# An audio front end on one core: layer 1 of its convolution stack with five products for two positions

## What is computed

```python
CONVS = [(128, 10, 5)] + [(128, 3, 2)] * 4 + [(128, 2, 2)] * 2     # channels, taps, stride
h = x[:, None, :]
for w, g, b, s in zip(conv_ws, ln_gs, ln_bs, strides):
    h = _conv1d(h, w, s)
    h = jnp.swapaxes(h, -2, -1)
    h = _fp32_layernorm(h, g, b)
    h = jnp.swapaxes(h, -2, -1)
    h = jax.nn.gelu(h, approximate=False)
```

## Time and profile before

| | |
|---|---|
| three runs | 2405.05, 2409.25, 2409.69 us; median 2409.25 |
| the profiled execution | 2401.78 us, span 2399.9 us |
| busy in the span | PE 2174.9 us (91%), DVE 1358.0 (57%), ACT 1133.1 (47%), POOL 861.3 (36%) |
| from 500 to 800 us | PE 297.08 us of 300, DVE 206.19, ACT 170.25, POOL 162.93; granted clock 1.00 |

### The profile page before, as it was taken

The page is one execution under the profiler, slowest core; times in us unless marked ns, Lnnn a source line. Parts: engine busy times, 40 slices in busy tenths (PEclk is TensorE's granted clock), DMA queues, the critical chain, the costliest instruction groups (busy, mean ns, idle before and its releaser), DMA issues. The chain is left out here.

```text
span 2399.9 us, 41759 instructions
## 1 busy us (share of the span) xinstructions
PE 2174.9 (91%) x14659; PEld 1945.7 (81%) x14659; DVE 1358.0 (57%) x3616; ACT 1133.1 (47%) x2203; POOL 861.3 (36%) x760
## 2 busy tenths in 40 slices
PE   2999999999999999999999995978697889969988
PEld 1888999999999998999999884977465566759988
DVE  4676667667667667667667652422486365542222
ACT  1655565655655565555555541322343465542320
POOL 4444555555555554554555531101330000000000
PEclk9999999999999999999999996999798799989989
DMA  5700000000000000000000202666000010119966
GB/s 160 238 4 4 4 4 4 6 7 4 8 6 4 7 6 4 9 6 4 9 4 1 65 1 73 188 166 176 20 20 0 26 52 39 52 41 329 331 202 222
DMA packets 102376, 150.39 MB, mean 63 GB/s; under 512 B 14724, under 2 KB 80174, under 8 KB 101548
## 3 DMA queue, kind: packets, MB, share of 16 engines
q1 hardware_dynamic: 78636, 118.36, 15.7%
q10 hardware_dynamic: 17984, 20.30, 2.6%
q0 software_dynamic: 5568, 9.27, 1.3%
HBM read 102.32 MB, written 45.50 MB: 62 GB/s over the span
## 5 line engine op out<-in xcount | busy, mean ns | idle before, releaser
L303 PE MATMUL banks<-t_wt,t_l 128*128 128x256 f32 (+1 forms) x2836 | 597.5, 350 | 0.0
L483 POOL TENSOR_TENSOR t_rstd<-t_var,t_minus_half 128x4 f32<-128x4 f32 (+1 forms) x379 | 367.1, 968 | 633.4 <-DVE t_var L412 632.0
L303 PEld LDWEIGHTS banks<-t_wt,t_l 128*128 128x128 f32 x2836 | 510.3, 192 | 51.9
L366 ACT ACTIVATE t_sq<-banks 128x512 f32<-128x512 f32 (+1 forms) x379 | 215.9, 570 | 560.4 <-PE banks L303 558.0
L420 DVE TENSOR_TENSOR t_yn<-banks,t_rstd 128x512 f32<-128x512 f32 (+1 forms) x379 | 249.0, 657 | 367.8 <-POOL t_rstd L483 366.7
L294 PE MATMUL banks<-t_wt,t_l 128*128 128x128 f32 x2836 | 385.7, 278 | 4.1 <-ACT t_l L384 2.9
L294 PEld LDWEIGHTS banks<-t_wt,t_l 128*128 128x128 f32 x2836 | 355.2, 193 | 13.8 <-ACT t_l L384 3.9
L489 POOL TENSOR_TENSOR t_zrstd<-t_zvar,t_minus_half 128x8 f32<-128x8 f32 x188 | 307.6, 1637 | 25.3 <-DVE t_zvar L447 25.3
L400 ACT ACTIVATE t_l<-banks,t_cols 128x512 f32<-128x512 f32 x376 | 286.4, 777 | 43.2 <-PE banks L356 39.7
L384 ACT ACTIVATE t_l<-banks,t_cols 128x512 f32<-128x512 f32 (+1 forms) x381 | 284.8, 747 | 13.6 <-PE banks L316 8.3
L409 DVE TENSOR_REDUCE t_ss<-t_sq 128x4 f32<-128x512 f32 (+1 forms) x379 | 244.6, 645 | 80.9 <-ACT t_sq L366 74.0
(11 more groups left out here) (330 smaller groups left out, 3581.1 us busy)
## 6 DMA issues: line engine op xcount, KB each, us to landing
t_w<-in_w SPq DMA_DIRECT2D x64, 480.0 KB
t_w<-in_w SPq DMA_DIRECT2D x27, 576.0 KB, 5.1
ect<-t_ECT SPq DMA_DIRECT2D x16, 750.0 KB, 3.2
t_l<-in_w1a SPq DMA_DIRECT2D x27, 384.0 KB, 5.4
sorted_by_expert<-t_h SPq DMA_DIRECT2D x4, 2400.0 KB, 11.1
routed_by_expert<-t_h SPq DMA_DIRECT2D x4, 2400.0 KB, 17.7
t_ectb<-ect ACTq DMA_DIRECT2D x5, 1500.0 KB, 8.0
t_w1x<-in_w1x SPq DMA_DIRECT2D x64, 97.5 KB
```

The source lines that it names most:

```text
L303: mm = pe.matmul(psY[bank][:, t * C:end * C], src[:, at:at + P], weights[:, C:(1 + end - t) * C], start=False, stop=(t + 1 == n))
L366: act.activation(T["sq"][:, par, 0:n], psY[bank][:, 0:n], ACT.Square).then_inc(S["squared"], 1)
L483: pool.tensor_tensor(T["rstd"][:, par, 0:n], T["var"][:, par, 0:n], T["minus_half"][:, 0:n], ALU.pow)\
```

## The change

Layer 1 is written as y(m) = W1 o(m) + (W0+W2) e(m) + W0 (e(m-1) - e(m)) for an even tile of a pair, and the same with W2 (e(m+1) - e(m)) for the odd one. The product (W0+W2) e(m) serves both. So PE does five products of 128 columns for two tiles in place of six.

- POOL computes the differences of layer-0 tiles (`differences`, five parts per chunk into `dif`), ahead of the roots of g5, g6, g7 and of g0 and g1.
- PE writes the two shared products of a group to a `psL` bank, ACT copies them to SBUF (`read_shared`), DVE adds them into the group's `psY` bank in place (`add_shared`, ahead of the normalise of the group before).
- In g0 to g3 ACT does the gelu ahead of the square, which now waits for the addition.
- The small DVE instruction that makes the variance goes: the squares are scaled on ACT, and epsilon stands in a 129th column that the sum takes in.
- `STEP_AT` has other places; `v` has room for two batch entries, with two waits for scatters.

```diff
 def conv(pe, j, g):
+    if g < WG:
+        pair_products(pe, j, g)
...
+def pair_products(pe, j, g):
+    for p in range(2):
+        at = tap(1, out_blocks(1, half)[2 * p], 2)
+        mm = pe.matmul(psL[par][:, p * C:(p + 1) * C], T["l0"][:, at:at + P], T["wsum"][:, :], start=True, stop=True)
+    mm.then_inc(S["shared_done"], 1)
+    pe.wait_ge(S["normed"], count(j, g) - BANKS)
+    pe.wait_ge(S["dif_ready"], 5 * j + (3, 3, 4, 5)[g])
+    for t, m in enumerate(out_blocks(1, half)):
+        o, at = psY[bank][:, t * C:(t + 1) * C], tap(1, m, 1)
+        pe.matmul(o, T["l0"][:, at:at + P], T["wt"][:, 0, :], start=True, stop=False)
+        mm = pe.matmul(o, T["dif"][:, half, t * P:(t + 1) * P], T["wt"][:, 2 - t % 2, :], start=False, stop=True)
...
 def stats(dve, e):
-    dve.reduce_sum(T["ss"][:, par, 0:n], T["sq"][:, par, 0:n * C].rearrange("p (t c) -> p t c", c=C), axis=AX.X)\
-        .then_inc(S["summed"], 1)
-    dve.wait_ge(S["summed"], number)
-    dve.tensor_scalar(T["var"][:, par, 0:n], T["ss"][:, par, 0:n], 1.0 / C, EPS, ALU.mult, ALU.add)\
-        .then_inc(S["var_ready"], 1)
+    dve.reduce_sum(T["var"][:, par, 0:n], T["sq"][:, par, 0:n, :], axis=AX.X).then_inc(S["summed"], 1)
...
+def read_shared(act, j, g):
+    act.wait_ge(S["shared_done"], sums(j, g))
+    act.activation(T["shared"][:, par, :], psL[par][:, 0:2 * C], ACT.Copy).then_inc(S["shared_read"], 1)
...
+def add_shared(dve, j, g):
+    dve.wait_ge(S["shared_read"], sums(j, g))
+    dve.wait_ge(S["conv_done"], number)
+    dve.tensor_tensor(y, y, shared, ALU.add).then_inc(S["added"], 1)
...
-STEP_AT = [-1, 0, 1, -1, 2, 3, 4, -1, 5, 6, 7, 8, 9, 10, 11, 12, -1, 13, 14, 15, -1, 16, 17, 18, -1, 19, 20, 21, 22, 23, -1, 24, 25,
+STEP_AT = [0, -1, 1, -1, 2, 3, 4, -1, 5, 6, 7, -1, 8, 9, 10, -1, 11, 12, -1, 13, 14, 15, 16, 17, 18, -1, 19, 20, 21, 22, 23, 24, 25,
...
         for j in range(CHUNKS):
             for g in range(NG):
+                if g < 2:
+                    differences(pool, j, g + 2)
+                if g >= 5 and j + 1 < CHUNKS:
+                    differences(pool, j + 1, (0, 1, 4)[g - 5])
                 root(pool, event(j, g))
```

More of the change, by code:

```diff
@@ L205, in _ @@
                 .then_inc(S["wt_centred"], 1)
+            dve.wait_ge(S["wt_centred"], 1)
+            dve.wait_ge(S["w0_split"], 1)
+            dve.tensor_tensor(T["wsum"][:, :], T["wt"][:, 1, :], T["wt"][:, 2, :], ALU.add)
         @block.tensor
@@ L352, in layer0 @@
             pe.wait_ge(S["patch_copied"], 2 * c + i // 4 + 1)
-        if not isinstance(c, int) or 8 * c + i >= 2:
+        if c >= 1 and i < 2:
+            pe.wait_ge(S["shared_read"], sums(c - 1, 2 + i))
+        if 8 * c + i >= 2:
             pe.wait_ge(S["l0_ready"], 8 * c + i - 1)
@@ L361, in square @@
     def square(act, e):
-        layer, _, bank, par, number, _ = e
+        layer, half, bank, par, number, _ = e
         n = tiles(layer) * C
-        act.wait_ge(S["conv_done"], number)
+        if layer == 1:
+            act.wait_ge(S["added"], sums(number // NG - 1, half))
+        else:
+            act.wait_ge(S["conv_done"], number)
         act.wait_ge(S["summed"], number - 2)
-        act.activation(T["sq"][:, par, 0:n], psY[bank][:, 0:n], ACT.Square).then_inc(S["squared"], 1)
+        act.activation(T["sq"][:, par, 0:tiles(layer), 0:C], psY[bank][:, 0:n].rearrange("p (t c) -> p t c", c=C), ACT.Square,
+                       scale=C ** -0.5).then_inc(S["squared"], 1)
     def gelu(act, e, carry=None):
@@ L480, in root @@
         n = tiles(layer)
-        pool.wait_ge(S["var_ready"], number)
+        pool.wait_ge(S["summed"], number)
         pool.wait_ge(S["normed"], number - 2)
@@ L484, in root, with differences @@
             .then_inc(S["rstd_ready"], 1)
+    def differences(pool, j, part):
+        l0 = T["l0"]
+        out = T["dif"][:, part % 4, :].rearrange("p (t c) -> p t c", c=P)
+        even = lambda m: l0[:, block_at(0, m):block_at(0, m) + P]
+        if part == 0:
+            pool.wait_ge(S["conv_done"], count(j - 1, 3))
+        pool.wait_ge(S["l0_ready"], 8 * j + (1, 3, 5, 7, 7)[part])
+        if part == 4:
+            at = block_at(0, POS - 2) - 1
+            pool.tensor_tensor(out[:, 0, :], l0[:, at:at + P], even(0), ALU.subtract).then_inc(S["dif_ready"], 1)
+            return
+        if part == 0:
+            pool.tensor_tensor(out[:, 1, :], even(2), even(0), ALU.subtract)
+            pairs, o = view(l0[:, :], [[4 * BLOCK, 2], [1, P]], block_at(0, 2)), out[:, 2:4, :]
+            middle = view(l0[:, :], [[0, 2], [1, P]], block_at(0, 4))
+        else:
+            pairs = view(l0[:, :], [[4 * BLOCK, 2], [4 * BLOCK, 2], [1, P]], block_at(0, 8 * part - 2))
+            middle = view(l0[:, :], [[4 * BLOCK, 2], [0, 2], [1, P]], block_at(0, 8 * part))
+            o = out.rearrange("p (a b) c -> p a b c", a=2)
+        pool.tensor_tensor(o, pairs, middle, ALU.subtract).then_inc(S["dif_ready"], 1)
     def patch_root(pool, c, part):
@@ L1458, in _ @@
                     patch_root(pool, c, part)
+            for part in (0, 1, 4):
+                differences(pool, 0, part)
             for j in range(CHUNKS):
                 for g in range(NG):
+                    if g < 2:
+                        differences(pool, j, g + 2)
+                    if g >= 5 and j + 1 < CHUNKS:
+                        differences(pool, j + 1, (0, 1, 4)[g - 5])
                     root(pool, event(j, g))
```

71 lines of the change are left out of this document (51 added, 20 removed).

## The result

The changed kernel takes 2463.24 us (median of four runs, 2462.46 to 2469.31) against 2408.06 before: a ratio of 1.0236, interval 1.0216 to 1.0256, or 55 us slower. I had forecast 2428, with a range of 2396 to 2458. The profiled execution took 2462.60 us with a span of 2460.8, so 61 us more than the one before, where my sum said 19.

What follows compares the result with a forecast made beforehand. DVE and POOL handing work to and fro would bind: five periods +17 us, first six chunks +2, last three +1.5, two bare chunks -1.5, sum +19, so 2421 us profiled and a median of 2428 (8 in 10: 2396 to 2458).

Steps and rivals of the forecast that it cites:

- my sum: Whole profiled execution: all stretches of the loop together +19 us, from 2401.8 to 2421 us.
- the bare chunk: A chunk of the loop without chain steps: 25.76 us, against 26.52 before.
- So I charge nothing: ACT's copy and square and DVE's addition lie in the shadow of POOL's root: no cost.
- The loop through DVE and POOL: Eight gaps between POOL's roots in a chunk without chain steps: 25.32 us, the hold not included.
- the subtractions: POOL's differences of layer-0 tiles: 1.25 us for 512 columns, 1.05 us for part 0.
- the hold: DVE's second half of split_patches waits for POOL's part 2 of the differences, both reading SBUF: 0.44 us a chunk.
- PE's 24.8 us: PE's own work in a chunk without chain steps after the change: 24.8 us, below the DVE and POOL loop.
- The first chunks: Stretches ahead of chunk 14: +0.5 us up to g7 of chunk 7, 0 in chunks 8 to 13.
- 25 of the 33 us: Chain steps' DVE and POOL work per six chunks is 33 us, of which 25 lengthen the loop: 179.6 us a period.
- The last three chunks, with a chain step in every group, +1.5: Chunks 44 to 46 at the end of the loop: 1.5 us longer than before.
- PE stays the bound: Rival: cheaper subtractions keep the loop hidden, up to 83 us won, 2326 us; 0.15 for a gain in part or whole.
- heavier: Rival: addition 0.2 us longer (+17) and subtractions with 0.1 us overhead (+9), 2454 us, more going past 2460; chance 0.10.

Runs made afterwards that it cites:

- 4 columns: The changed kernel with each part of the differences from the second chunk on cut to one instruction of 4 columns, layer 1 not computed: 2372.92 us.
- the filler: The changed kernel with useless PE products at two places of every six chunks where its clock fell by half after a wait: 2457.84 us.
- Putting the differences ahead: The changed kernel with each difference straight behind the root or patch_root of the group before, ahead of that group's chain step on POOL: 2439.97 us.
- the twelve units: The changed kernel with the two shared products of a group done twice, so PE does as many units as before the change: 2479.41 us.

## Why the prediction was wrong

The direction was right, and so was the bare chunk, but the size was too small by a factor of three in the profiled execution (61 us for 19), mainly because a wait was left out: "So I charge nothing" for the addition. By its steps:

- *The loop through DVE and POOL*, *the subtractions*, *the hold*: right, 25.81 us for 25.76 in a bare chunk, each part within 0.05 (the eight gaps add up to 25.31, not 25.32). The page of the Trainium skill that I cited (SBUF — State Buffer, "Who interferes with whom") agrees here: 1.61 or 0.95 for 0.48.
- *PE's 24.8 us*: 0.3 too low (busy for 25.1 of 25.4 with 4 columns), but it did not bind.
- *The first chunks*: 1.8 and 2.0 us more than said. The root of g4 in the first chunk already stands 1.6 us later (80.18 for 78.54), and I had charged nothing for the setup; no run looks into that. In chunks 8 to 13 the fifth takes 31.4, as in the later periods where the clock fell.
- **"So I charge nothing" for the addition**: this step failed. I priced the addition by its 0.69 us, which it takes, and looked for cover in bare chunks alone. But it also waits, for PE's products of the next group, and on PE these stand behind the products of a chain step; the normalise of the present group stands behind the addition.
- **The chain, "25 of the 33 us"**: too small by this wait. A period took 183.2 us (915.80 / 5) for 179.6, so the chain costs 28.4 over six bare chunks of 25.8. In the third, fifth and sixth chunk, where the 3.6 us lie, the normalise starts 1.76, 2.2 to 2.5 (where the clock had fallen) and 1.8 to 2.1 us behind its root and not 1.04. Summed over the five periods, what exceeds 1.04 is some 12 of the 18 us: an estimate from these rows. The hold adds 3 by the same reckoning: in the third chunk it is 1.13 us (1.61 for 0.48), not 0.44. The rest is not attributed. That the fifth chunk's share goes by the addition is shown by the filler (its wait and 1.5 us go together); for the other two it is read from the trace and no run takes it away. Putting the differences ahead gave 11.6 us back, but half of it in the first chunk, whose 33.7 us the forecast had.
- **"The last three chunks, with a chain step in every group, +1.5"**: the same wait, with less cover. They took +20.0 us. The differences' place gave back 3.3 and the rest of the five-product form 17.4 (together 20.7; the chunks then take 0.7 less than before the change). The waits of the addition for PE, 20.5 us in all, are what the trace shows for the larger part; the half clock that goes with them is in these figures, and no run parts the two.

Of the rivals, *PE stays the bound* is refuted by the twelve units (+16 us for 83 of PE's work), and *heavier* gave nearly the time, but by longer instructions, which did not occur. None of them had a wait of DVE for PE.

## What to carry to other kernels

When an instruction is put ahead of another on an in-order engine, price what it waits for, not only how long it takes, and do so in the stretch with the least cover: the addition was hidden in a bare chunk and waited 20.5 us in the three densest ones. Work handed to an engine that shares its row with rare long steps belongs ahead of those steps if a third engine waits for it. A saving on the busiest engine is worth only what the next loop leaves; doing it in half of the groups, with the differences ahead of the chain steps and not at all in the three densest chunks, won 14 us (2405.09 to 2390.96). Doing it in all groups with the same two precautions lost 20, and without them 55.

## What the runs showed of the hardware

- The hold between POOL and DVE did not come with every instruction of POOL. Beside POOL's subtractions, DVE's instruction with two SBUF operands took 0.95 at the median (L519, 0.48 before); beside POOL's power instructions, which also read SBUF, DVE's subtractions of 128, 256 and 512 columns took 0.28, 0.42 and 0.68 without a spread. The page of the Trainium skill (SBUF — State Buffer, "Who interferes with whom") names any GpSimd instruction that reads SBUF; here the measurement decides, for DVE instructions that start 0.4 us or more behind POOL's. The power instructions have 8 columns and the subtractions 128 to 512, so whether it goes by the operation or by the columns stays open.
- The same subtraction of 512 columns takes 1.27 us on POOL and 0.68 on DVE.
- PE's granted clock fell to half (1.2 GHz) behind waits of 2 to 3 us in the periods, for some 3 us each time, and several times in the last three chunks, once for 13 us (1426 to 1439). In the filler run it fell once behind 1.4 us of products only 4 columns wide (L691 and L692, from 628.47 to 629.89), with PE at work.
